# Output projection of a cross-attention block: 32-bit product replaced by three products of 16-bit halves

## The reference, cut to what matters

```python
# x: (8, 128, 512), ctx: (8, 2048, 512), all weights (512, 512), float32; 16 heads of 32
q = layernorm(x) @ Wq.T;  k = ctx @ Wk.T;  v = ctx @ Wv.T       # split into heads
attn = softmax(q_h @ k_h.T / sqrt(32))
heads = concat_h(attn @ v_h)                                     # (8, 128, 512)
x = x + heads @ Wo.T                                             # the output projection
# then: x += quantised self-attention(layernorm(x)); x += experts(layernorm(x))
```

## Time and profile before

| | |
|---|---|
| median of 3 runs | 1725.7 us (1724.34 to 1726.32) |
| span of the profiled execution | 1727.4 us (the page gives no other time of that execution) |
| TensorE matmul busy | 1628.6 us, 94% |
| VectorE busy | 1171.3 us, 68% |
| ScalarE busy | 767.5 us, 44% |
| GpSimd busy | 471.1 us, 27% |
| cross-attention | 0 to about 1127.9 us |
| self-attention | to about 1264 us |
| experts | to the end |

### The profile page before, as it was taken

The page is one execution under the profiler, slowest core; times in us unless marked ns, Lnnn a source line. Parts: engine busy times, 40 slices in busy tenths (PEclk is TensorE's granted clock), DMA queues, the critical chain, the costliest instruction groups (busy, mean ns, idle before and its releaser), DMA issues. The chain is left out here.

```text
span 1727.4 us, 39816 instructions
## 1 busy us (share of the span) xinstructions
PE 1628.6 (94%) x17264; PEld 1111.9 (64%) x17264; DVE 1171.3 (68%) x1400; ACT 767.5 (44%) x973; POOL 471.1 (27%) x412
## 2 busy tenths in 40 slices
PE   6999999999999999999999999896669999999998
PEld 4666666666666766666666666674447777777775
DVE  5678567457657757656766757557787767666766
ACT  5354336344444444435434533545445444344441
POOL 2323322232123123212222237632025411101133
PEclk9999999999999999999999999997879999999999
DMA  6544243334234233242233225460048655555544
GB/s 246 124 110 111 60 116 87 62 88 122 47 87 110 60 87 87 52 111 72 67 82 95 74 59 138 121 232 2 2 138 263 214 188 180 196 174 186 180 129 121
DMA packets 102151, 202.04 MB, mean 117 GB/s; under 512 B 25739, under 2 KB 25739, under 8 KB 101850
## 3 DMA queue, kind: packets, MB, share of 16 engines
q1 hardware_dynamic: 91258, 169.49, 34.1%
q0 software_dynamic: 10720, 30.02, 6.3%
HBM read 127.36 MB, written 18.90 MB: 85 GB/s over the span
## 5 line engine op out<-in xcount | busy, mean ns | idle before, releaser
L656 DVE TENSOR_REDUCE mx<-sc 128x4 f32<-128x2048 f32 x128 | 293.2, 2290 | 67.0 <-PE sc L900 66.4
L861 PE MATMUL proj<-w_hi,ctx 128*128 128x256 f16 x2048 | 273.7, 278 | 12.8 <-ACT ctx L441 12.6
L489 ACT ACTIVATE stage_w<-sc 128x1024 f32<-128x1024 f32 x256 | 248.2, 1024 | 70.8 <-PE sc L935 70.2
L875 PE MATMUL proj<-ctx,w_hi 128*128 128x512 f16 x1024 | 253.6, 380 | 0.0
L861 PEld LDWEIGHTS proj<-w_hi,ctx 128*128 128x128 f16 x2048 | 193.0, 99 | 64.6 <-issue 40.4
L452 ACT ACTIVATE stage_w<-proj 128x512 f32<-128x512 f32 x128 | 76.4, 597 | 340.8 <-PE proj L861 340.8
L383 POOL TENSOR_TENSOR acc_g<-stage_w 128x1024 f32<-128x1024 f32 x31 | 74.0, 2389 | 477.0 <-ACT stage_w L489 476.9
L678 DVE TENSOR_TENSOR acc_v<-acc_v,stage_w 128x1024 f32<-128x1024 f32 x93 | 131.9, 1418 | 87.1 <-ACT stage_w L489 84.3
L616 DVE SCALAR_TENSOR_TENSOR k_lo<-proj,k_hi 128x512 f16<-128x512 f32 x128 | 88.0, 687 | 118.6 <-ACT k_hi L461 117.7
L1166 DVE SCALAR_TENSOR_TENSOR w_lo<-stage_w,w_hi 128x2048 f16<-128x2048 f32 x64 | 144.8, 2293 | 34.2 <-ACT w_hi L1160 34.2
L875 PEld LDWEIGHTS proj<-ctx,w_hi 128*128 128x128 f16 x1024 | 90.1, 98 | 116.5 <-issue 25.1
(11 more groups left out here) (354 smaller groups left out, 2488.8 us busy)
## 6 DMA issues: line engine op xcount, KB each, us to landing
stage_w<-in_w SPq DMA_DIRECT2D x64, 1024.0 KB, 5.9
ctx_stage<-in_ctxT SPq DMA_DIRECT2D x64, 512.0 KB, 4.6
stage_w<-k_hi SPq DMA_DIRECT2D x256, 128.0 KB, 2.4
stage_w<-k_lo SPq DMA_DIRECT2D x128, 128.0 KB, 2.4
wq_f<-in_wiT POOLq DMA_DIRECT2D x24, 256.0 KB, 4.4
xg<-xbuf POOLq DMA_DIRECT2D x28, 176.0 KB, 4.4
obuf<-o_sb POOLq DMA_DIRECT2D x28, 176.0 KB, 3.5
xbuf<-final SPq DMA_DIRECT2D x17, 256.0 KB
```

The lines of the kernel that those rows point to most:

```text
L489: act.activation(probs[:, u % 4, :], unit_scores(u), ACT.Exp, scale=1.0 / sqrt(HD)).then_inc(e_ready, 1)
L656: dve.tensor_reduce(mx[:, :, kb], sc[:, :, :], AX.X, ALU.max).then_inc(m_read, 1)
L861: last = pe.matmul(out, x_part[:, kb, e, col:col + P], w_part[:, 2, e, wv], start=term == 0 and e == 0, stop=term == 2 and e == EC - 1)
L875: last = pe.matmul(proj[at % 2][:, :], w_part[:, 1, e, P * (g % G):P * (g % G) + P], x_part[:, kb, e, :], start=term == 0 and e == 0, stop ...
```

## The change

`wo` is loaded into `acc_v` and `acc_g` (two transfers), split by ScalarE and VectorE into `wo_hi` and `wo_lo`, which lie in the bytes of the old `wo`. `finish_group` writes the normalised heads times 16 into `rden`, then their high half and their low half, which lie in the bytes of the old `ot`. Each projection is 12 products of float16 in place of 4 of float32. The additions to `x1` multiply by 1/(1024*16) on the way. `ot_ready` is now counted by the product into `rden`, and a new semaphore `ot_split` by the low half.

```diff
+        wo_hi, wo_lo, ot_hi, ot_lo = out_views(wo, ot)
...
-                sp.dma_start(wo[:, :, :], woT.rearrange("(c p) d -> p c d", p=P)).then_inc(wo_in, 16)
+                for n, half in enumerate((acc_v, acc_g)):
+                    sp.dma_start(half.rearrange("p (c d) -> p c d", c=2),
+                                 woT.rearrange("(c p) d -> p c d", p=P)[:, 2 * n:2 * n + 2, :]).then_inc(wo_in, 16)
...
# GpSimd and VectorE, before the first sums of group 0 of batch 0
+                                gp.wait_ge(w_lo_ready, 5)
...
+                            dve.wait_ge(w_lo_ready, 5)
...
# ScalarE, between empty_bank(-1, LAST_V + 6) and split_q(0)
+                act.wait_ge(wo_in, 32)
+                for n, half in enumerate((acc_v, acc_g)):
+                    act.activation(wo_hi[:, 2 * n:2 * n + 2, :], half.rearrange("p (c d) -> p c d", c=2), ACT.Copy,
+                                   scale=WSCALE).then_inc(w_hi_ready, 1)
...
# VectorE, finish_group
+                    if b or g:
+                        dve.wait_ge(ot_split, 4 * b + g)
...
+                    dve.scalar_tensor_tensor(rden[:, :], po[:, 0:T], OSCALE, rden[:, :], ALU.mult, ALU.mult).then_inc(ot_ready, 1)
+                    dve.wait_ge(ot_ready, 4 * b + g + 1)
                     if g == 0 and not (isinstance(b, int) and b == 0):
                         dve.wait_ge(o_ready, b)
-                    dve.tensor_tensor(ot[:, g, :], po[:, 0:T], rden[:, :], ALU.mult).then_inc(ot_ready, 1)
+                    steps.did(dve.tensor_copy(ot_hi[:, g, :], rden[:, :]))
+                    steps.wait()
+                    dve.tensor_tensor(ot_lo[:, g, :], rden[:, :], ot_hi[:, g, :], ALU.subtract).then_inc(ot_split, 1)
...
# VectorE, before split_q(0)
+                for n, half in enumerate((acc_v, acc_g)):
+                    dve.wait_ge(w_hi_ready, 3 + n + 1)
+                    dve.scalar_tensor_tensor(wo_lo[:, 2 * n:2 * n + 2, :], half.rearrange("p (c d) -> p c d", c=2), WSCALE,
+                                             wo_hi[:, 2 * n:2 * n + 2, :], ALU.mult, ALU.subtract).then_inc(w_lo_ready, 1)
...
# add_x, and in the same way the last batch's addition (L1427)
-                    dve.tensor_tensor(x_b, misc[:, :], x_b, ALU.add).then_inc(x1_ready, 1)
+                    dve.scalar_tensor_tensor(x_b, misc[:, :], 1.0 / (WSCALE * OSCALE), x_b, ALU.mult, ALU.add).then_inc(x1_ready, 1)
...
# TensorE
                 def project_out(b):
-                    pe.wait_ge(ot_ready, 4 * b + 4)
+                    pe.wait_ge(ot_split, 4 * b + 4)
                     pe.wait_ge(row_set, 4 * b + 5)
-                    for g in range(G):
-                        last = pe.matmul(misc[:, :], ot[:, g, :], wo[:, g, :], start=g == 0, stop=g == G - 1)
-                    last.then_inc(o_ready, 1)
+                    project_heads(pe, misc[:, :], wo, ot).then_inc(o_ready, 1)
...
-                pe.wait_ge(wo_in, 16)
+                pe.wait_ge(w_lo_ready, 5)
...
+def out_views(wo, ot):
+    wo16 = wo.rearrange("p c d -> p (c d)").bitcast(f16).rearrange("p (a c d) -> p a c d", a=2, c=EC)
+    ot16 = ot.rearrange("p g t -> p (g t)").bitcast(f16).rearrange("p (a g t) -> p a g t", a=2, g=G)
+    return wo16[:, 0], wo16[:, 1], ot16[:, 0], ot16[:, 1]
+
+def project_heads(pe, bank, wo, ot):
+    wo_hi, wo_lo, ot_hi, ot_lo = out_views(wo, ot)
+    n_mm = 0
+    for o_part, w_part in mm_terms(ot_hi, ot_lo, wo_hi, wo_lo):
+        for g in range(G):
+            last = pe.matmul(bank, o_part[:, g, :], w_part[:, g, :], start=n_mm == 0, stop=n_mm == 3 * G - 1)
+            n_mm += 1
+    return last
...
# TensorE, self-attention stage, the last batch
-                for g in range(G):
-                    last = pe.matmul(pb[:, 0, :], ot[:, g, :], wo[:, g, :], start=g == 0, stop=g == G - 1)
-                last.then_inc(vx_ready, 1)
+                project_heads(pe, pb[:, 0, :], wo, ot).then_inc(vx_ready, 1)
```

More of the change, by code:

```diff
@@ L163, in cross_attention @@
         wo_in = sem("wo_in")
+        ot_split = sem("ot_split")
         w_in = [sem(f"w_in{i}") for i in range(3)]
@@ L382, in body @@
                                 gp.wait_ge(group_done, 4 * b + g)
+                            else:
+                                gp.wait_ge(w_lo_ready, 5)
                             gp.tensor_tensor(acc_g[:, :], probs[:, 2, :], probs[:, 3, :], ALU.add).then_inc(sum_g, 1)
@@ L813, in _ @@
                 body(0, False, steps)
-                FIRST_STEPS = steps.n
-                PER = 2 * G
                 weight_steps = Steps(dve, wq_step, 1)
                 for b in range(1, B - 1):
-                    loop_steps = Steps(dve, v_step, FIRST_STEPS + PER * (b - 1))
-                    body(b, False, loop_steps)
-                    assert loop_steps.n == PER
+                    body(b, False, steps)
                 dve.wait_ge(wmax_moved, 32)
@@ L826, in _ @@
                 dve.reciprocal(wq_inv[:, :], wscale[:, :]).then_inc(wq_scaled, 1)
-                last_steps = Steps(dve, v_step, FIRST_STEPS + PER * (B - 2))
-                body(B - 1, True, last_steps)
-                finish_group(B - 1, 3, last_steps)
+                body(B - 1, True, steps)
+                finish_group(B - 1, 3, steps)
             @block.tensor
@@ L1123, in _ @@
                 gp.wait_ge(made, 3)
+OSCALE = 16.0
+def out_views(wo, ot):
[10 more added lines that the diff above has]
+    return last
 E_, F = 8, 2048
@@ L1426, in _ @@
                 dve.wait_ge(vx_ready, 1)
-                dve.tensor_tensor(x1[:, B - 1, :], pb[:, 0, :], x1[:, B - 1, :], ALU.add).then_inc(vx_read, 1)
+                dve.scalar_tensor_tensor(x1[:, B - 1, :], pb[:, 0, :], 1.0 / (WSCALE * OSCALE), x1[:, B - 1, :],
+                                         ALU.mult, ALU.add).then_inc(vx_read, 1)
                 dve.wait_ge(vx_read, 1)
```

## The result

The changed kernel takes 1713.35 us, the median of 4 runs (1712.23 to 1717.5), beside 1725.02 us of the kernel before (4 runs, 1721.54 to 1726.32). The ratio is 0.9937, 95% interval 0.9919 to 0.9955: 11.7 us less, where the prediction had 6.7 less and a range that ended at 1716.0.

What follows compares the result with a forecast made beforehand. TensorE was taken to bound the kernel (94% busy; 133.04 of 135.00 us in one batch). Terms: -7.3 for projections, +0.6 at the barrier, -6.7 us in all; from 1725.7 to 1719.0 us, range 1716.0 to 1723.0.

Steps and rivals of the forecast that it cites:

- The products: Output projections on TensorE: each falls from 3.49 to 2.58 us, 0.91 us shorter; eight of them give 7.3 us less.
- That the gain arrives: Behind each projection in cross-attention: TensorE starting 0.91 us earlier meets no late partner, so the gain is kept.
- `finish_group`: VectorE's added copy and subtraction: 0.60 us a group, hidden in 31 of 32; the last, before the barrier, costs 0.6 us.
- The start: Loading and splitting the weight `wo` before `q_hi`: cost 0; 0.3 us if `wo` lands 2 us late.
- The barrier: TensorE's idle time at the barrier after the last `finish_group` grows by 0.6 us, from 1.68 to 2.3 us.
- the first rival: Longer idle time at the barrier brings low clock to transposes and projection behind it: about 3 us lost, 1722.0 us; chance 8%.
- The clock falls at the barrier: TensorE drops to half speed behind the barrier's 2.3 us idle time: about 3 us lost, 1722.0 us; chance 8%.
- The gain is swallowed: A partner of TensorE, such as the stacked keys, is late by what was saved; only +0.6 remains, 1726.3 us; chance 6%.
- VectorE becomes the bound: In group 2 VectorE's added 0.60 us gets through at seven turns and the clock may fall: +7.7, 1733.4 us; chance 3%.
- More than forecast: Stall on stacked keys at 334.14 shrinks, or low clock after 144.32 stays away: 1.7 to 3 us more gain, 1716.5; chance 7%.

Runs made afterwards that it cites:

- the split alone: Kernel before, with the copy and subtraction added to each `finish_group` into a buffer nobody reads, projections still 32-bit: 1727.38 us, ratio 1.0006.
- the three 32-bit products: Kernel before with three of the four 32-bit products in seven of the projections, the last four heads left out: 1715.28 us, ratio 0.9947.

## Why the prediction was wrong by its size

**What held.** *The products:* 0.91 us forecast, 0.90 in the timeline and 0.87 in the undisturbed period. *That the gain arrives:* taken from the first to the seventh projection, less the stall on the keys and less 1.67 for each turn at half clock and what stands behind the keys, the four traces of before have 805.9 to 806.6 us and the four of after 801.1 to 801.3. The 5.2 us between them are six times 0.87. *`finish_group`:* 0.60 forecast, 0.59 measured, and hidden in 31 of 32; the split alone costs nothing that can be told. *The start:* free. The two halves of the weight fit in front of `q_hi`, which starts 0.3 us earlier than before:

```profile
35.71 1.05 ACT L549 ACTIVATE wo_sb<-acc_v 128x1024 f16<-128x1024 f32 x1
36.66 1.05 ACT L549 ACTIVATE wo_sb<-acc_g 128x1024 f16<-128x1024 f32 x1
37.89 0.60 ACT L526 ACTIVATE q_hi<-misc 128x512 f16<-128x512 f32 x1 [0.19 <-PE misc L1030]
```

*The barrier:* 2.3 us forecast, 2.34 measured.

**The step that failed** is a sentence in the first rival: "A stall of 1.9 us in every later batch is not followed by one". It is, in four of six batches of the very trace that I had. I had looked at the wait in one batch and at the clock in a single turn, that of batch 2, one of the two that are spared, and wrote what I saw of one as a rule for all. The window of one batch at a clock of 0.99 should have made me ask where its missing hundredth lies: a stretch of 3.4 us at half clock takes 1.7 of 135 us, 1.3%, and that window holds the stretch from 695 to 698. From that sentence it followed that half clock was no term of the sum, except in one projection and as a risk of the change: what the change does to it at all other places was put at nothing. In truth the kernel before loses 12.4 us to it in the mean of its four traces, and the changed one 7.3.

So the sum has two terms more. Over four traces each, the mean spans are 1723.7 and 1711.4 us, 12.3 apart. Half clock accounts for 12.4 - 7.3 = 5.1 (a little less where TensorE is idle in such a stretch, as in the 0.95 us before 334.14), the shorter stall on the keys for 2.23 - 1.57 = 0.7, and 6.5 are left for the forecast's own terms, which had 6.7. The two terms together are 5.8 us, about the distance from the forecast, 1719.0, to the measured 1713.35.

**The rivals.** *The clock falls at the barrier*, given 8%: it happens in 2 of 4 traces of after, and behind an idle time of 2.34 us in 6 of 8 traces over all kernels that have it; behind 1.68 or 1.75 us in none of ten. The chance was put too low, for the same reason: I believed 1.9 us to be safe. Nor does the length of the wait order the cases: the 2.95 us at batch 0's turn, which I used as the yardstick, are followed by half clock in 7 of the 15 traces that have them. Its price was 1.7 us and not 3. *The gain is swallowed* and *VectorE becomes the bound* did not come: the wait in group 2 went from 1.92 to 1.95. *More than forecast* named the stall at 334.14 and the stretch behind batch 0's turn as what could add to the gain. Both did their part in the mean of the four traces: 0.7 us of stall and 1.7 of half clock at the keys, 0.9 behind batch 0's turn. The 2.6 at the other turns and the 0.9 in the last group it did not name, and its 7% was far too low. The Trainium skill, "TensorE: Matmul & The Clock Gate", section "What's actually happening", says that the throttled state is the default and that activity releases it. The traces agree: half clock comes behind idle times, of 1.9 us too, and ends while the engine works. I used this rule for the one gap that the change made longer, and not for those already there.

**What is shown, and what stays open.** Shown is that the changed kernel loses less to half clock, 3.2 us over the whole program in 12 executions against 78, and 5.1 in cross-attention in four traces against four. (In three of the four traces the changed kernel has one stretch more in self-attention, among waits of 2.4 to 3.5 us.) Shown is too that float16 products do not prevent it: four more of them bring the whole time back, half clock included. And where the wait at the turn is 0.86 to 0.89 us, no turn has half clock behind it. That the length of the projection is what counts rests on the added products, which cost 8.1 and 12.2 us for 3.0 and 6.0 of own time, on the three 32-bit products, and on counts at the turns, 23 of 42 against 8 of 42. The stretches of one trace need not be independent of each other, so the count is weaker than it looks. Why the length of a projection some 85 us earlier should matter for a turn whose own wait is unchanged, and what decides which turns of one execution are hit, stays open; no experiment was made for it. That the smaller loss behind the keys comes from the change, and not from four lucky traces (1.57 us of stall in the mean of them, but 2.33 and 2.45 in two variants), is not shown either.

## What to carry to other kernels

Where a kernel runs at 94% of TensorE, list the granted clock behind every repeated wait, over all batches and if possible over several executions, before a sum is made: a wait that is the same in each batch may cost 1.7 us more in some of them. In such a kernel a microsecond taken from TensorE, or from a wait in front of it, can be worth one and a half to two: 11.7 for 6.7 here, 9.1 for 6.1, 14.0 for 7.4, but only 6 to 8 for the same 7.4 in the changed kernel. An edit that adds 0.6 us of idleness can cost its own length several times in one execution (0.6 and 1.7); over several, taking it away again brought nothing that could be told. When a float16 split replaces a 32-bit product, price it by the starts of neighbouring records (0.87 us against 3 x 0.215), and look for the one place where VectorE's added copy has no cover.

## What the runs showed of the hardware

- An idle time of TensorE of 1.9 us is enough for 3.4 us at half clock behind it, but not each time: 14 of 24 turns of the kernel before. 2.95 us at batch 0's turn: 7 of 15. 2.34 us at the barrier: 6 of 8. 1.75 us or less at the barrier: none of 10. 0.75 to 0.89 at the turns: none of 18. Short waits that come close together are no such safe case: in the last group before the barrier, where several of 0.6 to 1.1 us lie within 8 us (1103.71 to 1111.41 in the kernel before), 3.4 or 6.8 us of half clock follow in all 18 traces.
- The stretch does not start with the first instruction after the gap: at 280.74 and 281.07 full clock still holds, and it falls within the products at 281.95, 1.2 us on. In the 22 cases of the two kernels it is 0.3 to 1.5 us.
- The same executable lies between 1719.8 and 1730.4 us over 12 runs of the kernel before. Its traces with spans of 1720.0 and 1727.4 us differ by 6.8 us of half clock and 2.4 of stall on the keys: what a median of few runs catches of these is most of its noise.
- A broadcast and two weight loads on GpSimd's queue beside the stacking of keys on SyncE's make the latter 1.2 to 3.6 us late for TensorE; put 5 us later, they make no stall (two traces).
